# Attention inside a macaron block: rotations placed behind the maxima, and the encoding's product added by GpSimd

## The reference

```python
x = x + 0.5 * ffn(layernorm(x))          # 64 experts, top 8, and a shared expert
x = x + attn(layernorm(x))
x = x + 0.5 * ffn(layernorm(x))

# attn: x is (8, 256, 128); 16 heads of 64
q, k, v = heads(x @ w_qkv.T)
fenc = fourier @ w_fproj.T + b_fproj      # (256, 64), the same for every batch and head
q = q * cos + rotate_half(q) * sin + fenc
k = k * cos + rotate_half(k) * sin + fenc
attn = softmax(einsum('bhid,bhjd->bhij', q, k) * 64 ** -0.5)
out = einsum('bhij,bhjd->bhid', attn, v) @ w_out.T + b_out
```

## Time and profile before

| | us |
|---|---|
| median of 3 runs | 913.99 (912.68 to 914.81) |
| the profiled execution's own time | 914.71 |
| its span, first to last instruction | 912.7 |
| start of the first round's `scores` | 294.57 |
| start of the last round's `scores` | 651.53 |
| rounds of the eight batches, from `scores` to `scores` (the last: seven rounds) | 43.16, 45.63, 45.94, 46.30, 46.10, 46.35, 45.84, 37.64 |

### The profile page before, as it was taken

The page is one execution under the profiler, slowest core; times in us unless marked ns, Lnnn a source line. Parts: engine busy times, 40 slices in busy tenths (PEclk is TensorE's granted clock), DMA queues, the critical chain, the costliest instruction groups (busy, mean ns, idle before and its releaser), DMA issues.

```text
span 912.7 us, 18913 instructions
## 1 busy us (share of the span) xinstructions
PE 850.9 (93%) x6328; PEld 745.5 (82%) x6328; DVE 568.5 (62%) x1736; ACT 503.8 (55%) x1376; POOL 494.3 (54%) x536
## 2 busy tenths in 40 slices
PE   5989989999964999999999999999979999999977
PEld 4889989999963777777777777777679999999962
DVE  7947753333336878888888888877543376433446
ACT  4423333333321888888888888888832333333336
POOL 4156777777762222256666666666657354444440
PEclk9779999999995999999999999999999999999999
DMA  9947877776626890000000000000050588888756
GB/s 327 368 160 225 258 231 227 236 242 218 205 87 227 197 151 1 1 14 27 23 25 25 25 25 25 22 19 15 6 211 18 182 313 284 279 287 291 241 190 259
DMA packets 65150, 140.70 MB, mean 154 GB/s; under 512 B 10223, under 2 KB 37296, under 8 KB 63940
## 3 DMA queue, kind: packets, MB, share of 16 engines
q1 hardware_dynamic: 53316, 118.59, 39.9%
q0 software_dynamic: 11776, 21.39, 7.5%
HBM read 107.72 MB, written 35.56 MB: 157 GB/s over the span
## 4 chain that ended last, share of the span: by engine, by line
PE 62%; POOL 13%; issue 6%; DVE 5%; ACT 4%; DMA 4%; DVEq 0%; ACTq 0%; POOLq 0%; SPq 0%
PE ps L1387 12%; PE ps L1962 6%; POOL y_rows L589 6%; POOL f_xg L578 6%; PE ps L1987 6%; PE ps L1406 6%; PE ps L615 5%; PE ps L1974 5%; PE ps L72 4%; PE ps L1947 3%; PE ps L2002 3%; PE ps L73 2%; PE ps L74 2%; ACT at_prob L2263 2%; PE ps L655 2%
## 5 line engine op out<-in xcount | busy, mean ns | idle before, releaser
L1856 POOL TENSOR_TENSOR at_m<-at_m 128x512 f32<-128x512 f32 x64 | 81.5, 1274 | 147.8 <-DVE at_m L2079 147.8
L1181 POOL DMA_INDIRECT xs_rows<-xr,slots_of x128 | 127.4, 995 | 43.8 <-issue 32.1
L2263 ACT ACTIVATE at_prob<-ps,at_nmax 128x256 f32<-128x256 f32 x256 | 118.0, 475 | 39.2 <-DVE at_nmax L2086 38.8
L1365 POOL DMA_INDIRECT y_rows<-f_og,f_put x80 | 81.7, 1021 | 95.6 <-ACT f_og L1518 76.1
L878 DVE TENSOR_TENSOR f_ehid<-f_esil,ps 128x480 f32<-128x480 f32 (+1 forms) x80 | 50.8, 634 | 116.0 <-ACT f_esil L719 107.9
L1657 DVE TENSOR_TENSOR f_hid<-f_sil,ps 128x480 f32<-128x480 f32 (+1 forms) x80 | 50.7, 634 | 107.0 <-ACT f_sil L1511 100.4
L1387 PE MATMUL ps<-f_xgT,f_ring 128*128 128x160 f32 x768 | 115.0, 299 | 1.7 <-issue 1.7
L615 PE MATMUL ps<-f_xgT,f_ring 128*128 128x160 f32 x768 | 114.9, 299 | 0.2 <-issue 0.2
L719 ACT ACTIVATE f_esil<-ps 128x480 f32<-128x480 f32 (+1 forms) x80 | 44.4, 555 | 120.8 <-PE ps L615 120.8
L1511 ACT ACTIVATE f_sil<-ps 128x480 f32<-128x480 f32 (+1 forms) x80 | 44.4, 555 | 118.8 <-PE ps L1387 118.8
L1387 PEld LDWEIGHTS ps<-f_xgT,f_ring 128*128 128x128 f32 x768 | 107.0, 190 | 2.1 <-issue 2.1
(11 more groups left out here) (256 smaller groups left out, 1844.2 us busy)
## 6 DMA issues: line engine op xcount, KB each, us to landing
f_ring<-in_wexp SPq DMA_DIRECT2D x128, 576.0 KB, 4.6
y_rows<-zeros SPq DMA_DIRECT2D x16, 512.0 KB, 6.2
f_yt<-y_rows SPq DMA_DIRECT2D x4, 2048.0 KB, 8.5
at_yt<-y_rows SPq DMA_DIRECT2D x6, 1024.0 KB, 4.9
xs_rows<-at_blank SPq DMA_DIRECT2D x16, 342.5 KB, 10.0
f_xg<-xs_rows SPq DMA_DIRECT2D x16, 342.5 KB, 3.3
y_rows<-f_og,f_put POOLq DMA_INDIRECT x160, 2.7
y<-y_rows SPq DMA_DIRECT2D x4, 512.0 KB, 4.4
```

What stands on the lines that cost most here:

```text
L1181: nc.gpsimd.indirect_dma_start(xs_dram, bass.IndirectOffsetOnAxis(s.slots_of[:, t, k:k + 1], 0), s.xr[:, t, :], None, bounds_check=last_sl ...
L1365: nc.gpsimd.indirect_dma_start(ydram, bass.IndirectOffsetOnAxis(put[:, n:n + 1], 0), og[:, g, c, :], None, bounds_check=last_row, oob_is_e ...
L2263: mm = nc.scalar.activation(prob[:, p % 2, h, t, :], ps[:, SB + h, t * SEQ:(t + 1) * SEQ], ACT.Exp, bias=nmax[:, p % 2, h, t:t + 1], accum ...
```

## The change

It does five things.

1. The product of the Fourier features and `w_fproj` is made once, ahead of the rounds, in tokens by columns: two matmuls into bank `SB` and one copy by ScalarE to `enc`. GpSimd's `add` has a second addition, `m1 + enc`, behind a wait for its own first one. The two matmuls of line 1952 leave `turn`.
2. VectorE's `rotate` moves from the end of a round to behind the maxima, and is of the pair p + 2 instead of p + 3. GpSimd's `add` follows it.
3. `qkv` is split in `project_v` and `project_qk`. TensorE's round is now `scores`, `values`, `turn`, `turn_p`, `project`, `project_v`, the router's product, `project_qk`.
4. ScalarE's round is now `exps`, `take_o`, `take_qk`, `take_p` of head 0, the router's copy, `take_p` of head 1, `normalise`, `take_v`.
5. The router's products use bank `SB`, between this round's `exps` of head 0 and the next round's `scores`, which therefore wait for the router's copy. The bias of the next batch's residual moves from round 3 to round 5 (`LN_BIAS`), and two waits on `vp` become waits on `qk`.

```diff
+        enc = sb("enc", [P, TPB * QKW])
+        half_sum, enc_w, enc_in = sem("half_sum"), sem("enc_w"), sem("enc_in")
-        LN_STATS, LN_MEAN, LN_APPLY, LN_BIAS = 0, 1, 2, 3
+        LN_STATS, LN_MEAN, LN_APPLY, LN_BIAS = 0, 1, 2, 5
...
                     nc.gpsimd.tensor_tensor(m1[:, p % 2, :], m1[:, p % 2, :], m2[:, p % 2, :],
+                                            ALU.add).then_inc(half_sum, 1)
+                    pool.wait_ge(half_sum, u + 1)
+                    nc.gpsimd.tensor_tensor(m1[:, p % 2, :], m1[:, p % 2, :], enc[:, :],
                                             ALU.add).then_inc(msum, 1)
...
-                        if there(b, p, -AHEAD, False, last):
-                            add(*pair(b, p, AHEAD))
+                        if there(b, p, 1 - AHEAD, False, last) and not (first and p == 0):
+                            add(*pair(b, p, AHEAD - 1))
...
-                    for half in range(2):
-                        mm = nc.tensor.matmul(ps[:, TB, half * SEQ:(half + 1) * SEQ], wfs[:, half * P:(half + 1) * P],
-                                              ffs[:, :], start=False, stop=(half == 1), skip_group_check=True)
...
                 def room(b, p):
                     u = PAIRS * b + p
-                    pe.wait_ge(vev, min(u + AHEAD, PAIRS * BATCH) if isinstance(u, int) else u + AHEAD)
-                    pe.wait_ge(oev, u - VLAG)
-                    return ps[:, VB, 0:TPB * P]
+                    pe.wait_ge(ex, 2 * u + 1)
+                    return ps[:, SB, 0:TPB * P]
...
+                        if p == 1 and kind in (MIDDLE, LAST):
+                            pe.wait_ge(s.room_r, 3 * (b - 2) + 3)
+                        if p == PICK_TURN + 1 and not first:
+                            pe.wait_ge(s.room_r, 3 * (b - 1) + 1)
+                        if p == PICK_LOGITS + 1 and not first:
+                            pe.wait_ge(s.room_r, 3 * (b - 1) + 2)
                         scores(b, p)
+                        if there(b, p, VLAG, first, last):
+                            values(*earlier(b, p, VLAG), ending)
+                        if there(b, p, -1, first, last):
+                            turn(*pair(b, p, 1))
+                        if there(b, p, 1, first, last):
+                            turn_p(*earlier(b, p, 1), 0, ending)
+                            turn_p(*earlier(b, p, 1), 1, ending)
+                        if there(b, p, JLAG, first, last):
+                            project(*earlier(b, p, JLAG), not last, not there_is_v)
+                        if p == LN_TURN and not last:
+                            turn_x(b + 1, False)
+                        if there_is_v:
+                            project_v(*nxt, xs)
...
+                        if there_is_v:
+                            project_qk(*nxt, xs)
...
+                        if there(b, p, 1 - AHEAD, first, last) and not (first and p == 0):
+                            rotate(*pair(b, p, AHEAD - 1))
                         invert(b, p, 0)
...
-                        if there(b, p, -AHEAD, first, last):
-                            rotate(*pair(b, p, AHEAD))
...
+                        if there(b, p, VLAG, first, last):
+                            take_o(*earlier(b, p, VLAG))
                         if there(b, p, -1, first, last):
                             take_qk(*pair(b, p, 1))
-                        if there(b, p, VLAG, first, last):
-                            take_o(*earlier(b, p, VLAG))
                         if there(b, p, 1, first, last):
                             take_p(*earlier(b, p, 1), 0)
+                        if p == PICK_TURN and not first:
+                            pick_take_x(nc, act, s, ps[:, SB, 0:TPB * P], b - 1)
...
+                for t in range(TPB):
+                    mm = nc.tensor.matmul(ps[:, SB, t * QKW:(t + 1) * QKW], ffs[:, t * P:(t + 1) * P], wfs[:, :],
+                                          start=True, stop=True)
+                mm.then_inc(enc_w, 1)
```

More of the change, by code:

```diff
@@ L1868, in batch @@
                 def batch(b):
-                    last = b == BATCH - 1
+                    first, last = b == 0, b == BATCH - 1
                     for p in range(PAIRS):
-                        if there(b, p, -AHEAD, False, last):
-                            add(*pair(b, p, AHEAD))
+                        if there(b, p, 1 - AHEAD, False, last) and not (first and p == 0):
+                            add(*pair(b, p, AHEAD - 1))
                         if p == LN_MEAN and not last:
@@ L1924, in qkv, with project_v @@
                     mm.then_inc(qk, 1)
+                def project_v(b, p, xs):
+                    u = PAIRS * b + p
                     taken = u - AHEAD - VLAG + 1
@@ L1946, in turn @@
                         for t in range(TPB):
[L1947 to L1950, removed]
-                    for half in range(2):
-                        mm = nc.tensor.matmul(ps[:, TB, half * SEQ:(half + 1) * SEQ], wfs[:, half * P:(half + 1) * P],
-                                              ffs[:, :], start=False, stop=(half == 1), skip_group_check=True)
+                            mm = nc.tensor.transpose(ps[:, TB, half * SEQ + t * P:half * SEQ + (t + 1) * P],
+                                                     m1[:, p % 2, t * QKW + half * P:t * QKW + (half + 1) * P],
+                                                     ident[:, :])
                     mm.then_inc(tq, 1)
@@ L1966, in scores, with turn_p @@
                                 mm.then_inc(sc, 1)
-                def turn_p(b, p, h):
+                def turn_p(b, p, h, alone=True):
                     u = PAIRS * b + p
                     pe.wait_ge(pn[h], u + 1)
-                    after(pe, pte, 2 * u + h - 1)
+                    if alone:
+                        after(pe, pte, 2 * u + h - 1)
                     for t in range(TPB):
@@ L2015, in batch @@
                     for p in range(PAIRS):
-                        scores(b, p)
+                        ending = last and p + AHEAD > PAIRS
+                        there_is_v = p + AHEAD < PAIRS or not last
+                        nxt, xs = pair(b, p, AHEAD), xcur if p + AHEAD < PAIRS else xnext
+                        if p == 1 and kind in (MIDDLE, LAST):
[4 more added lines that the diff above has]
+                            pe.wait_ge(s.room_r, 3 * (b - 1) + 2)
+                        scores(b, p)
+                        if there(b, p, VLAG, first, last):
[10 more added lines that the diff above has]
+                        if there_is_v:
+                            if p + AHEAD == PAIRS:
+                                pe.wait_ge(xx, b + 2)
+                            project_v(*nxt, xs)
                         if p == 0 and kind in (MIDDLE, LAST):
@@ L2022, in batch @@
                             pick_logits(nc, pe, s, room(b, p), b - 1)
[L2023 to L2033, removed]
-                        if there(b, p, VLAG, first, last):
[L2035 to L2045, removed]
+                        if there_is_v:
+                            project_qk(*nxt, xs)
                         if p == PAIRS - 1 and not last:
                             pe.wait_ge(xc, b + 2)
+                for t in range(TPB):
+                    mm = nc.tensor.matmul(ps[:, SB, t * QKW:(t + 1) * QKW], ffs[:, t * P:(t + 1) * P], wfs[:, :],
+                                          start=True, stop=True)
+                mm.then_inc(enc_w, 1)
                 turn_x(0, True)
                 pe.wait_ge(xx, 1)
-                qkv(0, 0, xnext)
-                qkv(0, 1, xnext)
+                project_v(0, 0, xnext)
+                project_qk(0, 0, xnext)
+                project_v(0, 1, xnext)
+                project_qk(0, 1, xnext)
                 turn(0, 0)
-                qkv(0, 2, xnext)
+                project_v(0, 2, xnext)
+                project_qk(0, 2, xnext)
                 pe.wait_ge(xc, 1)
@@ L2312, in batch @@
                             pick_exp(nc, act, s, b - 1)
+                act.wait_ge(enc_w, 1)
+                nc.scalar.copy(enc[:, :], ps[:, SB, :]).then_inc(enc_in, 1)
                 take_x(0)
```

19 lines of the change are left out of this document (9 added, 10 removed).

## The result

The changed kernel takes 991.71 us (median of 4 runs, 989.93 to 992.56) against 914.4; the ratio is 1.0842 (95% interval 1.0814 to 1.087), 8% slower. The forecast was 910.5 in a range up to 917.0.

A forecast was written before the change was run, and what follows sets the result against it. Bounds: TensorE's list and the loop through take_o, nearly coinciding. From 914.71: batches 2-6 -3.5, batch 1 -1.2, batch 0 -0.9, batch 7 -0.75 and +1.2, start +0.7, allowance +1.0, giving 911.2; median 0.7 lower: 910.5, range 904.5 to 917.

The forecast's parts named there:

- What the additions lie beside: GpSimd's additions beside VectorE's normalise and choice: contention costs GpSimd 0.3 us a round; middle batches taken as 45.4 us.
- above, the whole 1.3: Upper bound of that contention: additions share the whole 1.3 us of normalise and choice, costing 0.4 us.
- Loop 1, through take_o: Scores, maxima, exponentials, take_o, values' product, back to scores: sets an ordinary round at 5.48 us, a gain of 0.15.
- TensorE's list alone: TensorE's own work in a round without the encoding matmuls: 5.63 - 0.32 = 5.31 us.
- Loop 2, through take_v: TensorE's values waits for the previous round's take_v on ScalarE: 10.92 us for two rounds, 5.46 for one.
- the second rival: Wait on take_v replaces that on take_o; ScalarE stands 0.25 us for the second invert: 913.5 us, same; chance 0.23.
- The allowance: VectorE's second invert coming late for ScalarE's normalise of head 1: 1.0 us in all, between 0 and 3.
- GpSimd's occupancy: GpSimd in batches 2 to 6 with the second addition: 43.9 us of a 44.9 us batch, 1.0 of room.
- The router's products: Move to bank SB: no new bound in full rounds; batch 7's rounds 5 and 6 take 10.7 us together, +1.2.
- Ahead of the rounds: Before the first scores: values' product and second addition delay turn, encoding matmuls go: +0.7 us, between 0 and 2.

The follow-up runs named there:

- idle_add_2: Kernel before the change, plus a GpSimd addition nobody waits for, ahead of the round's own, in batches 0 and 1: 919.26 us, ratio 1.0062.
- add_behind_choice: Changed kernel with GpSimd's additions made to wait for VectorE's second invert, behind normalise and choice: 935.63 us, ratio 1.0237.
- early_encoding: Order of before, GpSimd adding the encoding to m1 beside VectorE's product with the sine, the two matmuls gone from turn: 916.56 us, ratio 1.0028.
- early_encoding_take_o: early_encoding with take_o ahead of take_qk in ScalarE's list: 912.8 us, ratio 0.9988.
- early_encoding_two_batches: early_encoding_take_o with GpSimd adding the encoding in batches 0 and 1 only, TensorE's two matmuls back from batch 2: 910.5 us, ratio 0.9968.
- adds_in_quarters: Changed kernel with each GpSimd addition cut in four pieces of 128 columns, no wait between them: 946.26 us, ratio 1.036.
- idle_copy: Kernel before the change, plus a GpSimd copy nobody waits for, behind the round's own addition, in batches 0 and 1: 914.09 us, ratio 1.0002.
- idle_copy_2: idle_add_2 with a GpSimd copy of 128 x 512 in place of the idle addition: 914.13 us, ratio 1.0006.
- enc_alone: Order of before, with the encoding added by GpSimd as a second addition: 928.8 us, ratio 1.0156.

## Why the prediction was wrong, point by point

- **The step that failed** is "What the additions lie beside". It had the place right (the additions start when normalise and choice begin) and both the payer and the price wrong. It priced the meeting as 0.3 us on GpSimd's additions, from a GpSimd copy that went from 0.29 to 0.42. What the runs showed: the additions stay at 1.28, and each VectorE instruction beside one waits to its end, 1.0 us more for each of normalise's two. Its upper bound, "above, the whole 1.3", was also put on GpSimd, where it would have cost only once a small room was used up; on VectorE 2 us a round come at once. The Trainium skill (SBUF — State Buffer, Who interferes with whom) states the shared port pair as an exclusive lock for a whole instruction, with whichever issues first blocking the other. The trace agrees: held instructions of normalise end 0.15 us behind the addition, and where normalise was ahead by 0.09 and 0.10 us (idle_add_2) it was the addition that took 1.37 to 1.40. A lead of 0.01 us by the profile's starts did not save normalise (30 cases in the changed kernel).
- **The same step, seen from before.** The source row of normalise had room for doubt that was not read: its mean in batch 4 was 0.395, though the same instruction takes 0.35 wherever nothing of GpSimd's lies beside it (35 of the 128 in that trace; the other 93 take 0.40, up to 0.62). And the copy that gave the price met the choice in two ways. Three times it took 0.42, having started 0.07 us behind a choice instruction of 0.33, which fits a wait for that short instruction. A fourth time it started 0.04 us behind, kept its 0.29, and the choice instruction took 0.47 and ended 0.14 us behind it:

```profile
398.66 0.73 DVE L2108 SCALAR_TENSOR_TENSOR x<-at_yt,wk,x  x2
398.70 0.29 POOL L1073 COPY gate<-gate_now 128x128 f32<-128x128 f32 x1
```

  The price of a meeting is the length of the other's instruction, not a rate; with the longer one on GpSimd's side it is VectorE's 1 us.
- **Loop 1, through take_o,** was right and a little long: 5.48 forecast, 5.40 measured where the hold is off (add_behind_choice). That this loop and not TensorE's list held the old round is shown by early_encoding (encoding off TensorE, 5.62) against early_encoding_take_o (5.24).
- **TensorE's list alone** was given as 5.31 without the encoding, taken from 5.63 with it. Both were too long, since the 5.63 held a wait. With take_o first, an ordinary round is 5.24 without the encoding and 5.49 with it (batch 4 of early_encoding_two_batches, scores below), so the two matmuls were worth 0.25, not 0.32:

```profile
477.14 1.14 PE L1978 MATMUL ps<-at_qkT 64*128 64x256 f32 x8
...
482.63 1.13 PE L1978 MATMUL ps<-at_qkT 64*128 64x256 f32 x8
```

- **Loop 2, through take_v,** is where the loss arrived, as the second rival had it: TensorE idle ahead of values, ScalarE idle ahead of normalise, 79.8 and 79.0 us. The rival's price was 0.25 us of waiting for the invert; it is 1.2 a round on average, 1.59 in the round shown.
- **The allowance** of 1.0 us for a late invert was mis-sized by the same hold.
- **GpSimd's occupancy,** 43.9 us a middle batch, was about right: 39.3 of work and 3.8 of DMA issue. It was never the bound of the changed kernel, since the round grew past it; in adds_in_quarters it was.
- **The router's products.** Rounds 5 and 6 of batch 7 were put at 10.7 together. They took 11.90 in the changed kernel, with the waits where they were expected, and 10.83 in add_behind_choice:

```profile
716.25 1.14 PE L1967 MATMUL ps<-at_qkT 64*128 64x256 f32 x8
...
722.44 1.14 PE L1967 MATMUL ps<-at_qkT 64*128 64x256 f32 x8 [1.12 <-ACT p_turned L1051]
...
728.15 1.13 PE L1967 MATMUL ps<-at_qkT 64*128 64x256 f32 x8 [1.26 <-ACT p_logits L1089]
```

- **Ahead of the rounds** +0.7 was forecast; the first scores come at 294.93 instead of 294.57, +0.4. Single traces differ by more here (292.35 in idle_copy, 294.55 in idle_copy_2), so the size is open; the cause is not. The first turn waits for the second addition, at 291.97 instead of 291.24:

```profile
291.97 1.11 PE L1956 MATMUL ps<-ident,at_m 128*128 128x128 f32 x4 [1.12 <-POOL at_m L1861]
```

Not shown: how the 77 us divide between the hold itself, the round's slack that it used up, and TensorE's lower clock behind it. The hold adds some 126 us to the length of VectorE's normalise in the rounds (174.7 against 48.9 us in sum); the rounds grew by 76.

## What to carry to other kernels

Before moving work to GpSimd, or a GpSimd instruction to another place in the round, look at what VectorE does beside it: an instruction like those held here (a product with a scalar, a copy or a cast from SBUF to SBUF, or one with two SBUF inputs; the cast took 1.3 us instead of 0.29 in add_behind_choice) stands until the GpSimd instruction has ended, however small it is, while one with a tensor from PSUM is not touched. An average of stretched instructions does not give a rate: see who started first, and what each ended behind. Place GpSimd's long instructions beside VectorE's PSUM work, and check every VectorE instruction of the stretch, not only the largest. And a matmul saved is worth nothing while a loop through other engines has the same length: open that loop with it.

## What the runs showed of the hardware that was not expected

- In the changed kernel the loss is all on VectorE's side: beside an addition of 1.28 us its instruction of 0.35 us takes 1.4 to 1.5, one of 0.17 us on two columns 1.26 (add_behind_choice), and the additions keep 1.26 to 1.33 (one took 1.44). With VectorE ahead it is the addition that is lengthened, to 1.37 to 1.45 (idle_add_2, early_encoding).
- A held instruction of normalise ends 0.15 us behind GpSimd's, whether that is an addition of 1.28, a piece of 0.47 or a copy of 0.61 us (changed kernel, adds_in_quarters, idle_copy_2).
- GpSimd's copy, with one input, holds it as well, for its 0.61 us.
- An instruction of VectorE's can be held beyond one GpSimd instruction: the longest normalise took 2.17 us. In one such case it started at 534.97, beside a scatter's issue that ended at 535.65, and the addition that followed at once, up to 536.96, held it on; it ended at 537.12.
- VectorE's instructions with PSUM as their tensor source, and one SBUF input at most, kept their 0.68 us beside the additions (48 products with the sine and 120 of the maxima in early_encoding). Nor is everything from SBUF to SBUF held: the reciprocal of two columns kept 0.16 to 0.17 us in all 55 cases in which it began well inside an addition (enc_alone).
